# The tail of a cross-attention and quantised FFN kernel: halves in place of whole steps and quarters, one step moved to ScalarE

## What is computed

```python
# attention block: 8 heads of 64
q = (layernorm(x) @ Wq); k = context @ Wk; v = context @ Wv
attn = softmax(q k^T / 8)
x = x + (attn v) @ Wout + bout
# FFN block, fake-quantised to 8 bits, I = 352
xq   = quant(layernorm(x))          # scale = sigmoid(clip) * max|.| / 127 over the whole tensor
gate = xq @ quant(w_gate).T;  up = xq @ quant(w_up).T
h    = quant(silu(gate) * up)       # again one scale from max|.| over the whole tensor
x    = x + h @ quant(w_down).T
```

## Time and profile before

| | before |
|---|---|
| median of 3 runs | 182.58 us (182.0 to 182.59) |
| the profiled execution: time | 182.32 us |
| the profiled execution: span | 180.3 us |
| busy share of the span | PE 96%, DVE 81%, ACT 74%, POOL 71% |
| chain that ended last | PE 89%, DVE 6% |
| HBM read / written | 10.97 MB / 0.23 MB |

### The profile page before, as it was taken

The page is one execution under the profiler, slowest core; times in us unless marked ns, Lnnn a source line. Parts: engine busy times, 40 slices in busy tenths (PEclk is TensorE's granted clock), DMA queues, the critical chain, the costliest instruction groups (busy, mean ns, idle before and its releaser), DMA issues.

```text
span 180.3 us, 2945 instructions
## 1 busy us (share of the span) xinstructions
PE 173.2 (96%) x890; PEld 143.1 (79%) x890; DVE 145.2 (81%) x341; ACT 133.7 (74%) x283; POOL 128.1 (71%) x137
## 2 busy tenths in 40 slices
PE   7999999999999999999999999999999999997782
PEld 3865678888888889888888898888888888896431
DVE  6496578969984896899988968999889779948784
ACT  3377999878869995778878857788777778756531
POOL 5697399989995887789887856899778664624010
PEclk9999999999999999999999999999999999999999
DMA  5678900180017000800081009000400000000001
GB/s 155 193 190 222 257 17 4 11 241 9 0 46 210 0 4 7 247 2 2 0 226 33 2 0 242 17 0 0 130 0 6 0 0 0 0 0 5 0 0 51
DMA packets 8331, 11.41 MB, mean 63 GB/s; under 512 B 4276, under 2 KB 6516, under 8 KB 8316
## 3 DMA queue, kind: packets, MB, share of 16 engines
q1 hardware_dynamic: 7900, 10.83, 22.9%
q10 hardware_dynamic: 416, 0.40, 0.8%
HBM read 10.97 MB, written 0.23 MB: 62 GB/s over the span
## 4 chain that ended last, share of the span: by engine, by line
PE 89%; DVE 6%; issue 1%; ACT 1%; POOL 1%; DVEq 0%; POOLq 0%
PE p_n L1054 11%; PE p_sw L1035 11%; PE p_m L1013 11%; PE p_n L1062 11%; PE p_sw L1027 11%; PE p_n L1056 11%; PE p_sw L1028 11%; PE p_n L963 3%; PE p_n L1070 1%; PE p_m L1130 1%; PE p_m L997 1%; PE p_n L997 1%; DVE h_flat L922 1%; PE p_sw L1130 1%; PE p_sw L977 1%
## 5 line engine op out<-in xcount | busy, mean ns | idle before, releaser
L369 POOL TENSOR_TENSOR e_lo<-e_full,e_hi 125x448 fp32r<-125x448 f32 x48 | 55.7, 1161 | 26.2 <-ACT e_full L541 25.1
L538 ACT ACTIVATE e_hi<-p_sw 125x448 fp32r<-125x448 f32 x96 | 52.2, 543 | 23.9 <-PE p_sw L1035 23.3
L674 DVE TENSOR_REDUCE chunk_max<-p_m 112x1 f32<-112x500 f32 x84 | 55.5, 672 | 16.3 <-PE p_m L1013 15.3
L1027 PE MATMUL p_sw<-q_hi,ctxT_lo 96*125 96x448 f32 x96 | 36.3, 378 | 0.0
L1054 PE MATMUL p_n<-e_hi,ctx_hi 125*128 125x448 f32 x96 | 35.5, 370 | 0.0
L1035 PE MATMUL p_sw<-q_hi,ctxT_hi 97*125 97x448 f32 x96 | 35.4, 368 | 0.0
L1028 PE MATMUL p_sw<-q_lo,ctxT_hi 96*125 96x448 f32 x96 | 35.1, 365 | 0.0
L1062 PE MATMUL p_n<-e_lo,ctx_hi 125*128 125x448 f32 x96 | 35.1, 365 | 0.0
L1056 PE MATMUL p_n<-e_hi,ctx_lo 125*96 125x448 f32 x96 | 35.0, 365 | 0.0
L689 DVE TENSOR_TENSOR e_lo<-p_n,e_hi 125x448 fp32r<-125x448 f32 x48 | 29.6, 616 | 4.0 <-ACT p_n L555 3.8
L1013 PE MATMUL p_m<-ctxT_hi,q_hi 96*112 96x500 f32 x84 | 32.1, 392 | 0.0
(11 more groups left out here) (248 smaller groups left out, 206.7 us busy)
## 6 DMA issues: line engine op xcount, KB each, us to landing
ctx_in<-ctx_d SPq DMA_DIRECT2D x8, 504.0 KB
ctxT_in<-ctxT_d SPq DMA_DIRECT2D x7, 562.5 KB, 5.8
ctxT_in<-ctxT_d SPq DMA_DIRECT2D x3, 187.5 KB, 4.6
ctx_in<-ctx_d SPq DMA_DIRECT2D x8, 58.5 KB
q_hi<-maxima SPq DMA_DIRECT2D x28, 0.4 KB, 1.9
wout<-wout_d SPq DMA_DIRECT2D x1, 256.0 KB, 7.2
wqkT<-wqkT_d SPq DMA_DIRECT2D x1, 224.0 KB, 4.7
wvT<-wvT_d SPq DMA_DIRECT2D x1, 192.0 KB, 6.6
```

Of the source, the lines that this page charges most:

```text
L369: pool.tensor_tensor(e_lo[:, k, :], e_full[:, k, :], e_hi[:, k, :], ALU.subtract)\
L538: act.activation(e_hi[:, k, :], p_s[n % 2][0:KT, 0:HQ], ACT.Exp, scale=SCALE)\
L674: dve.reduce_max(chunk_max[:, c // NM, c % NM:c % NM + 1], p_mb[c % NM][0:GQ, 0:MC], AX.X)\
L1027: pe.matmul(o, ctxT_lo[b % 2][:, keys], q_hi[0:C, b, :], start=True, stop=False)
```

## The change

All edits lie in the tail.
- VectorE's order for the denominators becomes: columns and reciprocal of the first half, columns of the second, row transpose of the first, reciprocal of the second. The scaling of four heads becomes two of two heads, and TensorE waits for each.
- The last pair is centred by ScalarE (Identity with scale 0.5 and the new `shift2`, minus half the mean, as bias), ahead of its weight copies; VectorE makes `shift2`. The late pair's maximum is taken after the last pair's statistics.
- The late pair's Newton step becomes one GpSimd instruction with two multiplies and one on VectorE; its combination with the maxima comes ahead of the last pair's Newton step. ScalarE scales the late pair between the second and the third weight copy.
- x: tokens 0 to 223 are quantised in one piece. Gate and up-projection of the first 128 columns come by halves of the tokens, gate, up, gate, up, in other PSUM banks; silu and product by halves too. One filler fewer stands ahead of them. The wait for the first silu moves from the third block's gate to the second's.
- h: the casts back to bf16 of the second and the third block, and the matmuls behind them, go by halves of the tokens.

```diff
-        g_banks = [p_s[0], p_s[1], p_x]
-        g0_banks = [p_x, p_s[0], p_o[1]]
+        g0_banks = [p_x, p_o[1]]
+        g_banks = [None, p_x, p_s[1]]
+        u0_banks = [p_mb[0], p_s[0]]
...
             pool.wait_ge(s.late_pow, 1)
-            pool.tensor_tensor(late_nt[:, :], late_rstd[:, :], late_rstd[:, :], ALU.mult).then_inc(s.late_pow, 1)
-            pool.wait_ge(s.late_pow, 2)
-            pool.tensor_scalar(late_nt[:, :], late_nt[:, :], late_veps[:, :], 3.0, ALU.mult, ALU.subtract)\
+            pool.tensor_scalar(late_nt[:, :], late_rstd[:, :], late_rstd[:, :], late_veps[:, :], ALU.mult, ALU.mult)\
                 .then_inc(s.late_pow, 1)
             pool.wait_ge(s.veps2_made, PAIRS - 1)
             pool.tensor_tensor(rstd2[:, :], veps2[:, :], minus_half[:, 0:1], ALU.pow).then_inc(s.pow2_made, 1)
-            pool.wait_ge(s.late_pow, 3)
-            pool.tensor_tensor(late_rstd[:, :], late_nt[:, :], late_rstd[:, :], ALU.mult).then_inc(s.late_pow, 1)
-            pool.wait_ge(s.late_pow, 4)
-
-            pool.wait_ge(s.silu_made, 4)
+
+            pool.wait_ge(s.silu_made, 3)
             pool.wait_ge(s.up2_made, 1)
...
             act.activation(warm[:, :], sig127[0:1, :], ACT.Silu)
+            act.wait_ge(s.shift2_made, 1)
+            act.activation(x1_now[:, :], p_x[0:TOK, 0:D], ACT.Identity, bias=shift2[:, :], scale=0.5)\
+                .then_inc(s.last_centred, 1)
             for k, dst in enumerate((wgT[:, :], wuT[:, :], wdT[:, :, :])):
                 src = p_mb[k].bitcast(BF16)
+                if k == 2:
+                    act.wait_ge(s.late_x_made, 1)
+                    act.wait_ge(s.late_pow, 3)
+                    act.activation(xh[:, PAIRS - 2, :], late_x[:, :], ACT.Copy, scale=late_rstd[:, :]).then_inc(s.late_xh_made, 1)
                 act.wait_ge(s.wT_made, k + 1)
                 if k < 2:
...
-            act.wait_ge(s.late_x_made, 1)
-            act.wait_ge(s.late_pow, 4)
-            act.activation(xh[:, PAIRS - 2, :], late_x[:, :], ACT.Copy, scale=late_rstd[:, :]).then_inc(s.late_xh_made, 1)
...
-            for k, cols in enumerate(QUARTERS + [others]):
+            for k, cols in enumerate(HALVES):
                 act.wait_ge(s.gate_made, k + 1)
                 act.activation(silu[:, 0, cols], g0_banks[k][:, cols], ACT.Silu, scale=xscale[:, 0:1])\
                     .then_inc(s.silu_made, 1)
...
-            act.activation(hq[:, 1, :], h8[:, 1, :], ACT.Copy).then_inc(s.h1_quantised, 1)
+            for cols in HALVES:
+                act.activation(hq[:, 1, cols], h8[:, 1, cols], ACT.Copy).then_inc(s.h1_quantised, 1)
...
                 columns(*halves[0])
+                invert(*halves[0])
                 columns(*halves[1])
-                invert(*halves[0])
+                rows(*halves[0])
                 invert(*halves[1])
-                rows(*halves[0])
                 dve.wait_ge(step[0], 2)
                 scale(0, 2)
                 scale(2, 2)
                 rows(*halves[1])
                 dve.wait_ge(step[1], 2)
-                scale(4, 4)
+                scale(4, 2)
+                scale(6, 2)
 
...
                 .then_inc(s.late_x_made, 1)
-            dve.wait_ge(s.late_x_made, 1)
-            dve.reduce_max(late_max[:, :], late_x[:, :], AX.X, apply_absolute_value=True).then_inc(s.late_step, 1)
-
             dve.wait_ge(s.projected, PAIRS - 1)
             dve.bn_stats(stats2[:, :], p_x[0:TOK, 0:D]).then_inc(s.ln2_step, 1)
             dve.wait_ge(s.ln2_step, 2 * PAIRS - 3)
             dve.bn_aggr(mv2[:, :], stats2[:, :]).then_inc(s.ln2_step, 1)
             dve.wait_ge(s.ln2_step, 2 * PAIRS - 2)
             dve.tensor_scalar(veps2[:, :], mv2[:, 1:2], EPS, None, ALU.add).then_inc(s.veps2_made, 1)
-            dve.tensor_scalar(x1_now[:, :], p_x[0:TOK, 0:D], mv2[:, 0:1], 0.5, ALU.subtract, ALU.mult)\
-                .then_inc(s.xmax_step, 1)
-            dve.wait_ge(s.xmax_step, 2)
+            dve.tensor_scalar(shift2[:, :], mv2[:, 0:1], -0.5, None, ALU.mult).then_inc(s.shift2_made, 1)
+            dve.wait_ge(s.late_x_made, 1)
+            dve.reduce_max(late_max[:, :], late_x[:, :], AX.X, apply_absolute_value=True).then_inc(s.late_step, 1)
+            dve.wait_ge(s.late_pow, 2)
+            dve.scalar_tensor_tensor(late_rstd[:, :], late_nt[:, :], 3.0, late_rstd[:, :], ALU.subtract, ALU.mult)\
+                .then_inc(s.late_pow, 1)
+            dve.wait_ge(s.last_centred, 1)
             dve.reduce_max(xmax1[:, :], x1_now[:, :], AX.X, apply_absolute_value=True).then_inc(s.xmax_step, 1)
-            dve.wait_ge(s.pow2_made, 4 * (PAIRS - 2) + 1)
-            newton_one(dve, rstd2[:, :], nt2[:, :], veps2[:, :], s.ln2_step, 2 * (PAIRS - 1))
-            dve.wait_ge(s.late_pow, 4)
+            dve.wait_ge(s.xmax_step, 1)
+            dve.wait_ge(s.late_pow, 3)
             dve.wait_ge(s.late_step, 3)
             dve.scalar_tensor_tensor(xmax[:, 2:3], late_max[:, :], late_rstd[:, :], xmax[:, 2:3], ALU.mult, ALU.min)\
                 .then_inc(s.late_step, 1)
-            dve.wait_ge(s.xmax_step, 3)
+            dve.wait_ge(s.pow2_made, 4 * (PAIRS - 2) + 1)
+            newton_one(dve, rstd2[:, :], nt2[:, :], veps2[:, :], s.ln2_step, 2 * (PAIRS - 1))
+            dve.wait_ge(s.xmax_step, 2)
...
-            own, others = HALVES
+            dve.wait_ge(s.xhT_made, 1)
+            dve.tensor_scalar(x8[:, own], xh_banks[0][:, own], xs[:, 2:3], None, ALU.mult).then_inc(s.xmax_step, 1)
             dve.wait_ge(s.xmax_step, 6)
-            dve.wait_ge(s.xhT_made, 1)
-            for k, cols in enumerate(QUARTERS):
-                dve.tensor_scalar(x8[:, cols], xh_banks[0][:, cols], xs[:, 2:3], None, ALU.mult).then_inc(s.xmax_step, 1)
-                dve.wait_ge(s.xmax_step, 7 + k)
-                dve.tensor_copy(xq[:, cols], x8[:, cols]).then_inc(s.x_quantised, 1)
-                if k == 0:
-                    dve.tensor_scalar(xscale[:, :], wscale[:, 0:6], xs[:, 1:2], None, ALU.mult).then_inc(s.xscale_made, 1)
+            dve.tensor_copy(xq[:, own], x8[:, own]).then_inc(s.x_quantised, 1)
+            dve.tensor_scalar(xscale[:, :], wscale[:, 0:6], xs[:, 1:2], None, ALU.mult).then_inc(s.xscale_made, 1)
             dve.wait_ge(s.x8_made, 1)
             dve.tensor_copy(xq[:, others], x8[:, others]).then_inc(s.x_quantised, 1)
...
-                multiply(0, cols, k + 1, 1)
-            multiply(2, own, 4, 2)
-            dve.wait_ge(s.h_made, 3)
+            for k, cols in enumerate(HALVES):
+                multiply(0, u0_banks[k], cols, k + 1, k + 1)
+            multiply(2, u2_banks[0], own, 3, 3)
+            dve.wait_ge(s.h_made, 2)
             dve.reduce_max(h_flat[:, 3 * ALLTOK:3 * ALLTOK + 1], hh[:, 0, :], AX.X, apply_absolute_value=True).then_inc(s.h_step, 1)
-            multiply(1, slice(0, ALLTOK), 5, 3)
-            dve.wait_ge(s.h_made, 5)
+            multiply(1, u_banks[1], slice(0, ALLTOK), 4, 4)
+            dve.wait_ge(s.h_made, 4)
             dve.wait_ge(s.last_h_made, 1)
             dve.wait_ge(s.h_step, 1)
             dve.reduce_max(hmax1[:, :], h_flat[:, ALLTOK:3 * ALLTOK + 1], AX.X, apply_absolute_value=True)\
...
-            for k, f in enumerate((0, 2)):
-                fn = FT[f][1]
-                dve.wait_ge(s.h_step, 3 + k)
-                dve.tensor_copy(hq[0:fn, f, :], h8[0:fn, f, :]).then_inc(s.h_quantised, 1)
+            dve.wait_ge(s.h_step, 3)
+            dve.tensor_copy(hq[:, 0, :], h8[:, 0, :]).then_inc(s.h_quantised, 1)
+            dve.wait_ge(s.h_step, 4)
+            for cols in HALVES:
+                dve.tensor_copy(hq[0:96, 2, cols], h8[0:96, 2, cols]).then_inc(s.h_quantised, 1)
...
-                    pe.wait_ge(s.last_attn_made, min(1 + h // 2, 3))
+                    pe.wait_ge(s.last_attn_made, 1 + h // 2)
...
-            busy(6, p_mb[1])
+            busy(5, p_mb[1])
...
-            for k, cols in enumerate(QUARTERS + HALVES[1:]):
+            for k, cols in enumerate(HALVES):
                 pe.wait_ge(s.x_quantised, k + 1)
                 pe.matmul(g0_banks[k][:, cols], wgT[:, 0:128], xq[:, cols], start=True, stop=True).then_inc(s.gate_made, 1)
-            up(0)
-            pe.wait_ge(s.silu_made, 1)
+                pe.matmul(u0_banks[k][:, cols], wuT[:, 0:128], xq[:, cols], start=True, stop=True).then_inc(s.up_made, 1)
+            pe.wait_ge(s.x8_made, 1)
             gate(2)
             for k in (1, 0):
                 last = pe.matmul(u2_banks[k][0:96, HALVES[k]], wuT[:, 256:F], xq[:, HALVES[k]], start=True, stop=True)
             last.then_inc(s.up_made, 1)
+            pe.wait_ge(s.silu_made, 1)
             gate(1)
-            up(1)
+            pe.matmul(u_banks[1][:, 0:ALLTOK], wuT[:, 128:256], xq[:, :], start=True, stop=True).then_inc(s.up_made, 1)
             pe.wait_ge(s.silu_made, 2)
-            busy(11, p_s[0])
+            busy(11, p_o[1])
             pe.wait_ge(s.hmax_ready, 1)
```

(71 more changed lines are left out.)

3 lines of the change are left out of this document (1 added, 2 removed).

## The result

The changed kernel takes 181.4 us (median of 14 runs), the kernel before, timed beside it, 182.06 (14 runs): ratio 0.9958, 95% interval 0.9946 to 0.997. That is 0.66 us or 0.4% faster by the medians; the interval leaves out 1, but the difference is under the half percent that the prediction asked of "faster", so it counts as the same. One of the 14 runs of the changed kernel took 186.44 us, in a slower state that the kernel before also showed once (187.14 us in a later call), and the ratio leaves such runs out. The single profiled spans differ by more (180.3 to 179.4 us), because the tail also began 0.21 us earlier in this execution (160.84 against 161.05).

The account below looks back on a forecast made before the run. A chain of TensorE matmuls bounds 161 us, then a single thread of engines taking turns for the last 19. Gains 0.12 + 0.16 + 0.27 + 0.12 = 0.67 us gave 181.65, named as 181.8; range 181.1 to 182.5.

Parts of the forecast that it names:

- the likeliest case: Whole kernel: the time counts as the same, within half a percent of the kernel before; chance 0.61.
- rival: Alternatives to the forecast gain: detour takes part back (0.15), more than forecast (0.15), table load (0.04), neither (0.06).
- more than forecast: Tail: first scaling not held, short centring, a whole activation saved, 0.20 at the end; gain 1.0, about 181.4 us; chance 0.15.
- Part 1: Denominators of the last batch up to its projection, half by half: 0.12 us gained, bounds 0 and 0.21.
- The hold: First scaling waits for the second reciprocal as well as the row transposition: 0.12 us gained, 0.21 if not held.
- Part 2: Last pair's statistics and maximum, from projection's end to the maximum's broadcast: 0.16 us net gain, bounds 0.05 and 0.23.
- P: End of the last projection (165.15 us in the kernel before), from which the last pair's steps are counted.
- the detour: Last pair's centring on ScalarE instead of VectorE: maximum 0.20 us later against the projection's end.
- Part 3: x and the first products by halves of the tokens: 0.27 us gained, bounds 0.07 and 0.37.
- The silu chain: ScalarE's activations after x: two of 112 columns become one of 224, one start fewer, 0.25 us shorter.
- Part 4: h and the output by halves: TensorE runs through its six matmuls, y 0.12 us earlier, bounds 0 and 0.20.

Follow-up runs that it names:

- the tiny read: Changed kernel plus one 32x1 VectorE copy from PSUM partition 0 after the second column transposition of the denominators; a single run, 181.96 us.
- part 1 undone: Changed kernel with the old order of the denominators and four heads scaled in one again; ratio 0.9981 to the kernel before.
- the run without it: Changed kernel with the last pair centred on VectorE from PSUM and the late pair's maximum in its old place; ratio 0.9967 to the kernel before.
- the run with one wait: Changed kernel with the wait for x1T's copy put ahead of the last filler, leaving the first gate matmul one wait; ratio 0.9952 to the kernel before.
- The kernel with reordered waits: Changed kernel with centring on VectorE, second reciprocal before the row transposition, latest wait written first on five instructions; 180.94 us, ratio 0.9926 to the kernel before.
- added instructions: Changed kernel with centring on VectorE, second reciprocal first, three second waits moved onto or ahead of fillers or a tiny activation; 181.15 us, ratio 0.9944.

## Why the prediction was right

The gain held: 0.67 us predicted, 0.67 by the traces, 0.66 by the medians; and it counts as the same, as the likeliest case said. That the total agrees to a hundredth is luck: the parts are off by 0.03, 0.02, 0.06 the other way and 0.01, and these nearly cancel. No rival came true. The time named for "more than forecast", 181.4, is the measured one, but for another reason: that rival needed a gain of 1.0. The time itself, 181.4, lies 0.4 below the 181.8 named, inside the range. The gain isn't at fault for that but its base: the kernel before measured 182.06 over 14 runs, the first three had 182.58. I had named 181.8, above the sum's own 181.65, to lean towards that median; 182.06 less 0.67 is 181.39. The border for "faster", 181.67, hung on the same base; half a percent below 182.06 is 181.15.

- *Part 1*, 0.15 for 0.12. The hold, taken from the gap between two reciprocals, was right, shown by the tiny read: scaling 0.10 earlier (0.12 put), and not held it would have been 0.17 (0.21 put). Both fall short because the row transposition starts 0.65 after the first reciprocal (161.29 to 161.94), where 0.61 was put. What was wrong is "the split of the last scaling gains nothing by itself". Before, the four-head scaling ended at 163.96, and the load of the fifth head's weights, due at 163.95, could start only at 164.02: TensorE paused there, and its 16 matmuls took 2.05, now 2.00. I had left this hand-over of 0.06 out. No run has the split alone; the pause is read from the traces, and it is there again with part 1 undone (2.05).
- *Part 2*, 0.18 for 0.16. All stages fell within 0.02 of the working: ScalarE's centring 0.37 for 0.35, maximum at P+1.24 (1.23), Newton at P+1.57 (1.58), broadcast at P+2.38 (2.40). That the detour costs was argued in the prediction and shown by the run without it. That run also leaves 0.33 for the order together with the new split, 0.32 put for the order. But the prediction called the new split of the third pair's Newton step worth nothing on the thread, and by row L425 above that is wrong in the new order, which would have waited for the old split; no run tried it. The sum was not touched, since both came together. The price of the detour was put at 0.20 against P; it is 0.14 at the broadcast, since GpSimd's power would bound next. The copies behind the centring stayed covered, as said: the first ended at 166.35, 0.8 before the broadcast.
- *Part 3*, 0.21 for 0.27. The silu chain gave 0.27, a little over the 0.25. Mis-sized was the hand-over from the cast to the gate: 0.06 put, 0.15 measured, for which the run with one wait accounts. In the kernel before, the price of the second wait can't be seen, since the sixth filler held the first gate back longer: it started at 169.59, 0.31 after its cast had ended (169.28).
- *Part 4*, 0.13 for 0.12. TensorE ran through its six matmuls as worked out.

The Trainium skill's rule on held instructions (VectorE: DVE Perf Modes, section Two Vector instructions with no wait between them) gave the right side of part 1. The runs now bear it out for a PSUM input too: 162.46 after 162.43 without the tiny read, 162.90 before 162.95 with it.

## What to carry to other kernels

In a tail where engines hand over to one another, most terms could be worked out to 0.03 us from start and end times (one hand-over was missed by 0.09), and they nearly add up (0.41 of 0.46); so ask of each edit whether it shortens the thread, not whether it moves work to an idle engine. The detour over ScalarE, with its two hand-overs, cost 0.14 us here although VectorE had two steps to fill the wait with; it still idled 0.17. Where an instruction has several waits, write the one that is fulfilled last first: here that and two moves on VectorE were worth 0.56 us more (first y at 15.04 against 15.60), nearly as much as the change itself.

## What the runs showed of the hardware that was not expected

- The order in which waits are written matters: where the one that is fulfilled last was written first, the instruction starts 0.04 to 0.06 us after it, where it was written later 0.10 (VectorE, ScalarE) or 0.15 (TensorE) after it, even if the others were long fulfilled. The kernel with reordered waits has the broadcast, the gate and the first silu where added instructions had put them (broadcast at 6.01 in both, silu at 8.15 and 8.16), and the products and the first y, reordered only there, bring another 0.15 (15.04 against 15.20).
- A VectorE instruction more can bring the next one forward: the 32x1 PSUM read made the scaling start 0.07 earlier.
- The tail repeats to 0.01 us from execution to execution while whole runs differ by 0.5 to 0.9. In the two profiled executions of the changed kernel the tail starts at 160.84 and 161.19 and the times are 181.43 and 181.77, so the spread arises before the tail; where in those 161 us was not tried.
